# Attention kernel: the sum of a row's squares over the channels as two float32r products with eight columns of weights, in place of one fp32 product

## The chip, the cores and the metric

The kernel runs on one core of a Trainium2 chip. The time is that of the device in microseconds (us), the median over several executions. An execution under the profiler gives the trace that the rows below are read from.

## What is computed

The input `x` has 8 rows of 512 tokens with 512 channels. Each row is layer-normed, goes through gated linear attention with 16 heads and then through a gated MLP, and is multiplied by a gate that a mixture of low-rank experts gives. What the change touches is the second normalization of the attention block:

```
def rmsnorm(x, w, eps=1e-05):
    return x * jax.lax.rsqrt(jnp.mean(x * x, axis=-1, keepdims=True) + eps) * w
...
x = x + o @ Wo
xn2 = rmsnorm(x, ln2_w)
x = x + jax.nn.silu(xn2 @ W1) * (xn2 @ W3) @ W2
```

The mean runs over the 512 channels of each token, here of `x + o @ Wo`.

## The kernel before

Three stages follow each other: F (normalization and experts), A (attention) and M (MLP). Each goes over the 8 rows; on every engine the stage is a first part, a loop and a last body. Activations lie with the channels on the partitions: 128 partitions by 4 blocks of channels by 512 tokens. Most large products are made of float32r operands split in a high and a low part (`..hi`, `..lo`; `product3` at L160 to L162 issues hi·hi, hi·lo, lo·hi). A few small ones are plain fp32; the trace records each of those as two MATMULs.

Stage A walks a row in four chunks of 128 tokens, `c` from 0 to 3. Every engine has its own copy of this order, written by hand, and waits for others on counting semaphores (`count.at(name, i)`: all of row `i`). Pieces of the next row are put between the chunks by `ahead("k0")`, `ahead("q1")` and so on. In the last row (row 7) these pieces are instead those of stage M's beginning (`Front`): for `c` = 3 on ScalarE `third_a`, and on VectorE `weights_lo(dve, 7, 9)` (L1520), which makes two low parts of MLP weights.

The mean of squares, in row `i` for the row before it (whose `x + o @ Wo` lies in `xn`):
- ScalarE squares the four channel blocks (L1190) during chunks 0 to 2, GpSimd adds them into `square` (L1107). `square` and `added` are the first two quarters of the buffer `cum`, under which name the trace shows them.
- TensorE, in chunk 3, after the q1 product of the next row and `variance(i, 2)` (L1303), multiplies `square` by `avg_all`, 128 by 128 with 1/512 everywhere (L1377), into the PSUM region `ms`. Of its 128 equal rows one is read.
- ScalarE makes the inverse root of one partition (`deviation`, L1194 and L1196), SyncE stores it.

Around it, in chunk 3: VectorE first applies the causal mask to both halves of the attention weights (L1022, two instructions), then, once ScalarE has made the inverse deviation of chunk 2, normalizes and gates that chunk's output (`gated`, L1063 to L1070), whose last two steps write the high and low parts `og_hl`. After L1377 TensorE goes on with the state products (L1390) and the products with the masked weights (L1399). The slices of `og_hl` for chunk 3 are free until `gated(i, 3)`, at the end of the row.

Of the kernel before, what the change touches and what calls it, by code (L numbers as in the profile page):

```python
# [5 lines left out]
F32 = mybir.dt.float32  # L6
F32R = mybir.dt.float32r
ALU = mybir.AluOpType
ACT = mybir.ActivationFunctionType
# [4 lines left out]
P = 128  # L14
# [760 lines left out]
def phase_a(nc, outer, consts, f, shared, w, xn_d, r1_d, xmid_d):  # L775
    ident, hmask, causal, avg32, avg_all, ones, eps = consts
    NB, _, KT, T = xn_d.shape
    D = KT * P
    KD = w["wkg2"].shape[1]
    GR = KD // P  # L780
    NC = T // P
# [6 lines left out]
    with ctx:  # L788
        def sb(name, shape, dt=F32):
            return ctx.enter_context(nc.sbuf_tensor("a_" + name, shape, dt))[:]  # L790

        def pair(name, shape):
            return [sb(name + part, shape, F32R) for part in ("hi", "lo")]
# [4 lines left out]
        xn, xa, gsilu = shared  # L798
# [21 lines left out]
        state = [sb(f"state{n}", [P, GR, HG * VH]) for n in range(2)]  # L820
        sq, oc, rn = sb("sq", [P, QD, P]), sb("oc", [P, QD, P]), sb("rn", [P, QD, P])
        og_hl = pair("og", [P, KT, T])
        v_tok = sb("v_tok", [P, NC, D])


        square, added = flat(cum)[:, 0:T], flat(cum)[:, T:2 * T]
# [2 lines left out]
        ps_att = [ctx.enter_context(nc.psum_tensor(f"a_att{n}", [P, 2, GR, 2, P], F32))[:] for n in range(2)]  # L829

        count = Counts(nc, outer, "a")
        for name, per in (("xa_in", 32), ("x2", KT), ("x2sum", KT - 1), ("r2", 1), ("r2_out", 16), ("xn_in", 16), ("xa", KT), ("xahi", KT), ("xalo", KT), ("uhi", 3),
                          ("absz", GR),
                          ("expz", GR), ("softz", GR), ("logg", GR), ("cum", GR * NC), ("offs", 3),
                          ("bias", 1), ("e64", 2), ("e32", 2), ("edk", 1), ("edq", 1), ("ekh", 1), ("eqh", 1),
                          ("decay", 1), ("m64", 3), ("m32", 3), ("mdk", 1), ("mdq", 2), ("mkh", 1), ("mqh", 1),
                          ("state", GR * (NC - 2)), ("first", NC - 1), ("weighing", NC),
                          ("sq", NC), ("rn", NC), ("og", 2 * NC), ("oghi", NC), ("oglo", NC)):
            count.add(name, per)
# [12 lines left out]
        dense = Regions(count, "dense", psum[0:3], sum((results for _, results in order), []), sum(early.values(), []))  # L852
        att = Regions(count, "att", ps_att, [f"{c}_{n}" for c in range(NC) for n in range(2)])
        mix = Regions(count, "mix", psum[3:4], list(range(NC)))
        LAST = KT - 1
        parity, s_parity = sb("parity", [P, 2]), outer.enter_context(nc.semaphore("a_parity"))
        w["ready"] = outer.enter_context(nc.semaphore("aw_ready"))

# [4 lines left out]
        def tokens(c):  # L863
            return slice(c * P, (c + 1) * P)
# [54 lines left out]
        def vector(dve, front):  # L919
# [76 lines left out]
            def clear():  # L996

                dve.tensor_tensor(parity, hmask[:, 0:2], hmask[:, 2:4], ALU.add).then_inc(s_parity, 1)
                dve.wait_ge(s_parity, 1)
                dve.tensor_tensor(parity, parity, hmask[:, 4:6], ALU.add).then_inc(s_parity, 1)  # L1000
                dve.wait_ge(s_parity, 2)
                dve.tensor_tensor(parity, parity, hmask[:, 6:8], ALU.add).then_inc(s_parity, 1)
                dve.wait_ge(s_parity, 3)
                dve.wait_ge(*f.turn.ready(f"xn{LAST}", NB - 1))
                dve.memset(u.bitcast(F32), 0.0)

            def clear_weights():
# [6 lines left out]
            def body(i, ahead):  # L1014
                ahead("split")
                for c in range(NC):
                    if c > 0:
                        dve.wait_ge(*mix.ready(c - 1, i))
                    for n in range(2):
                        dve.wait_ge(*att.ready(f"{c}_{n}", i))  # L1020
                        ps = att.region(f"{c}_{n}").rearrange("p s g o t -> p (s g o) t")
                        dve.tensor_tensor(a_sb[n].rearrange("p s g o t -> p (s g o) t"), ps, bcast(causal, 1, 4 * GR),  # L1022
                                          ALU.mult).then_inc(att.taken_sem(f"{c}_{n}"), 1)
                    ahead(("c0", "u", "c2", "c3")[c])
                    if c + 1 < NC:

                        new, old = state[(c + 1) % 2], state[c % 2]
                        dve.wait_ge(*dense.ready(f"ds{c}", i))
                        ds = dense.region(f"ds{c}")[:, 0:GR * 2 * VH].rearrange("p (g o v) -> p g o v", g=GR, v=VH)
                        for g in range(GR):  # L1030
                            ins = dve.tensor_tensor(new[:, g, :].rearrange("p (h o v) -> p h o v", o=2, v=VH),
                                                    bcast(ds[:, g], 1, HG // 2),
                                                    bcast(hmask.rearrange("p (h o) -> p h o", o=2), 3, VH), ALU.mult)
                            if g == 0:
                                ins.then_inc(count.sem("first"), 1)
                        ins.then_inc(dense.taken_sem(f"ds{c}"), 1)
                        if c > 0:
                            dve.wait_ge(*count.at("first", i, c + 1))
                            dve.wait_ge(*dense.taken(f"ds{c}", i))
                            dve.wait_ge(*count.at("decay", i))  # L1040
                            for g in range(GR):
                                gc = g * NC + c
                                dve.scalar_tensor_tensor(new[:, g, :], old[:, g, :],
                                                                        decay[:, gc:gc + 1], new[:, g, :],
                                                                        ALU.mult, ALU.add).then_inc(count.sem("state"), 1)
                            dve.wait_ge(*count.at("state", i, GR * c))
                    if c > 0:
                        gated(i, c - 1)
                ahead("gates")
                gated(i, NC - 1)  # L1050
                ahead("upper")
                ahead("last")
                ahead("decayed")
                dve.wait_ge(*count.at("xn_in", i))
                for m in range(KT):
                    dve.wait_ge(*dense.ready(f"o{m}", i))
                    dve.tensor_tensor(xn[:, m, :], dense.region(f"o{m}"), xn[:, m, :],
                                                          ALU.add).then_inc(dense.taken_sem(f"o{m}"), 1)
# [54 lines left out]
        def scalar(act, front):  # L1113
# [84 lines left out]
            def body(i, ahead):  # L1198
                ahead("split")
                for c in range(NC):  # L1200
                    if c + 1 < NC:
                        act.wait_ge(*dense.ready(f"kt{c}", i))
                        act.activation(flat(kt_sb), dense.region(f"kt{c}")[:, 0:GR * P],
                                                            ACT.Copy).then_inc(dense.taken_sem(f"kt{c}"), 1)
                    for part in (("k0", "k1"), ("c1",), ("q0",), ("q1",))[c]:
                        ahead(part)
                    if c == 0:
                        act.wait_ge(*dense.taken_before(f"o{LAST}", i))
                    squares(i, ((0, 1), (2,), (3,), ())[c])
                    if c > 0:  # L1210
                        inverse_deviation(i, c - 1)
                    if c == NC - 1:
                        deviation(i)
                    act.wait_ge(*mix.ready(c, i))
                    ps = mix.region(c)
                    act.activation(flat(sq), ps, ACT.Square).then_inc(count.sem("sq"), 1)
                    if c > 0:
                        act.wait_ge(*count.at("og", i, 2 * (c - 1) + 1))
                    act.activation(flat(oc), ps, ACT.Copy).then_inc(mix.taken_sem(c), 1)
                ahead("z")  # L1220
                ahead("v0")
                inverse_deviation(i, NC - 1)
                ahead("exponentials")
                ahead("g")
# [35 lines left out]
        def tensor(pe, front):  # L1260
# [95 lines left out]
            def body(i, ahead):  # L1356
                weights(i, 0)
                for c in range(NC):
# [14 lines left out]
                        variance(i, c - 1)  # L1373
                    if c + 1 == NC:
                        pe.wait_ge(*dense.free("ms", i))
                        pe.wait_ge(*count.at("x2sum", i))
                        pe.matmul(dense.region("ms"), avg_all, square, start=True, stop=True).then_inc(dense.ready_sem("ms"), 1)  # L1377

                    pe.wait_ge(*mix.free(c, i))
                    ps = mix.region(c).rearrange("p (q t) -> p q t", t=P)  # L1380
# [50 lines left out]
                        linear(0, "q", wq, xa_hl, m, first)  # L1431

            f.tensor(pe, first_row)
            for part in ("v0", "v1", "g"):
                parts[part](0)
            loop_parts(pe, NB, parts, body, skip=front.tensor(pe), first=False)
# [552 lines left out]
```

## Time and profile before

| | |
|---|---|
| median of 3 runs | 1624.28 us (1623.22 to 1626.05) |
| time of the profiled execution | 1622.4 us |
| its span in the trace | 1620.7 us |
| TensorE busy | 1593.2 us, 98% |
| VectorE, ScalarE, GpSimd busy | 52%, 35%, 10% |
| granted TensorE clock, mean | 0.998 of full |

A busy share is the part of the span in which the engine had an instruction in flight. The span is the trace's; the time around it is 1.7 us longer. A line number with an engine names a group of instructions; PEld is TensorE's loading of weights, which runs beside its products.

### The profile page before, as it was taken

Reading aid. Unit: us, or ns where it says so; the run is one execution under the profiler, and the core shown is the slowest. Engines: PE = TensorE matmul, PEld = TensorE weight load, DVE = VectorE, ACT = ScalarE, POOL = GpSimd, SP = SyncE. Lnnn points to the kernel's source line nnn. Section 1 sums busy time; section 2 is a strip of 40 time slices with the busy share of each in tenths; the row PEclk is TensorE's granted clock in tenths of the full one; section 3 lists DMA queues with packets and bytes.
Section 4 is the critical chain, followed back from the end, with each engine's and each line's share of the span. In section 5 each row is a group of like instructions: output and inputs, shape, how many; then the busy total and the mean of one; then the engine's idle time right before and its main releaser. Section 6 shows DMA issues by size and latency. Waiting matters only on the chain.

```text
span 1620.7 us, 30581 instructions
## 1 busy us (share of the span) xinstructions
PE 1593.2 (98%) x12274; PEld 1277.6 (79%) x12274; DVE 847.3 (52%) x1311; ACT 567.2 (35%) x982; POOL 167.2 (10%) x190
## 2 busy tenths in 40 slices
PE   7999999999999999999999999999999999999998
PEld 5777888777777777777777788888888888888886
DVE  5565455367797887978876451331415142241413
ACT  4333343366564645636564411111111111111111
POOL 4770000100220102101020000000000000000000
PEclk9999999999999999999999999999999999999999
DMA  7563332101020210202213423030301203030200
GB/s 175 151 135 78 83 95 69 59 27 52 9 84 0 84 53 32 84 0 84 84 54 118 144 101 127 0 136 0 136 0 49 87 0 136 0 136 0 91 14 26
DMA packets 50700, 113.16 MB, mean 70 GB/s; under 512 B 13321, under 2 KB 24665, under 8 KB 42466
## 3 DMA queue, kind: packets, MB, share of 16 engines
q1 hardware_dynamic: 47906, 99.95, 19.5%
q10 hardware_dynamic: 1152, 8.39, 1.3%
q0 software_dynamic: 1600, 4.25, 0.9%
q8 instruction: 28, 0.46, 0.1%
q14 instruction: 14, 0.11, 0.0%
HBM read 78.98 MB, written 33.59 MB: 69 GB/s over the span
## 4 chain that ended last, share of the span: by engine, by line
PE 94%; DVE 2%; ACT 1%; issue 1%; DMA 1%; PEld 0%; SPq 0%; ACTq 0%; DVEq 0%; PEldq 0%
PE m_ps L1529 10%; PE m_ps L1531 10%; PE m_ps L1530 10%; PE a_ps L160 7%; PE a_ps L162 7%; PE a_ps L161 7%; PE f_ps L160 5%; PE f_ps L162 5%; PE f_ps L161 5%; PE m_ps L1543 5%; PE m_ps L1544 5%; PE m_ps L1545 5%; PE a_att L1282 3%; PE a_ps L1399 2%; PE a_ps L1303 2%; PE a_ps L1390 1%
## 5 line engine op out<-in xcount | busy, mean ns | idle before, releaser
L1529 PE MATMUL m_ps<-m_xshi,m_w 128*128 128x512 f32 x680 | 268.1, 394 | 1.4 <-DVE m_w L1520 1.4
L1766 DVE TENSOR_TENSOR m_h<-m_ps,m_silu 128x512 f32<-128x512 f32 x85 | 58.7, 690 | 402.4 <-PE m_ps L1531 402.4
L1531 PE MATMUL m_ps<-m_xshi,m_w 128*128 128x512 f32 x680 | 266.5, 392 | 0.0
L1530 PE MATMUL m_ps<-m_xslo,m_w 128*128 128x512 f32 x680 | 266.4, 392 | 0.0
L1830 ACT ACTIVATE m_silu<-m_ps 128x512 f32<-128x512 f32 x85 | 50.8, 597 | 334.3 <-PE m_ps L1531 334.3
L1529 PEld LDWEIGHTS m_ps<-m_xshi,m_w 128*128 128x128 f32 x680 | 127.7, 188 | 30.0 <-issue 2.1
L1531 PEld LDWEIGHTS m_ps<-m_xshi,m_w 128*128 128x128 f32 x680 | 127.6, 188 | 28.7
L1530 PEld LDWEIGHTS m_ps<-m_xslo,m_w 128*128 128x128 f32 x680 | 127.7, 188 | 28.1 <-issue 0.2
L1101 POOL TENSOR_TENSOR row<-row,a_r 128x512 f32<-128x512 f32 x32 | 50.7, 1615 | 331.6 <-DMA a_r<-scratch_r 331.6
L1022 DVE TENSOR_TENSOR a_a<-a_att,causal 128x1024 f32<-128x1024 f32 x64 | 75.2, 1216 | 11.8 <-PE a_att L1282 11.8
L1839 ACT ACTIVATE m_h0hi<-m_h 128x512 fp32r<-128x512 f32 x46 | 29.1, 632 | 135.7 <-DVE m_h L1766 135.7
L1543 PE MATMUL m_ps<-m_h0hi,m_w 128*128 128x512 f32 x192 | 75.3, 392 | 0.0
L1544 PE MATMUL m_ps<-m_h0lo,m_w 128*128 128x512 f32 x192 | 75.3, 392 | 0.0
L1545 PE MATMUL m_ps<-m_h0hi,m_w 128*128 128x512 f32 x192 | 75.3, 392 | 0.0
L1839 ACT ACTIVATE m_h1hi<-m_h 128x512 fp32r<-128x512 f32 x39 | 24.7, 632 | 115.6 <-DVE m_h L1766 115.6
L1107 POOL TENSOR_TENSOR a_cum<-a_cum 128x512 f32<-128x512 f32 x24 | 30.7, 1281 | 321.3 <-ACT a_cum L1190 321.3
L1543 PE MATMUL m_ps<-m_h1hi,m_w 128*128 128x512 f32 x160 | 62.6, 391 | 0.0
L1544 PE MATMUL m_ps<-m_h1lo,m_w 128*128 128x512 f32 x160 | 62.6, 391 | 0.0
L1545 PE MATMUL m_ps<-m_h1hi,m_w 128*128 128x512 f32 x160 | 62.6, 391 | 0.0
L160 PE MATMUL f_ps<-f_xnhi,f_w1hi 128*128 128x512 f32 x128 | 52.1, 407 | 2.5 <-DVE f_xnlo L476 1.2
L160 PE MATMUL a_ps<-a_wvhi,a_xahi 128*128 128x512 f32 x128 | 53.1, 415 | 0.0
L160 PE MATMUL a_ps<-a_xahi,a_wghi 128*128 128x512 f32 x128 | 50.8, 397 | 0.9 <-ACT a_v_tok L1149 0.6
(306 smaller groups left out, 3487.9 us busy)
## 6 DMA issues: line engine op xcount, KB each, us to landing
row<-scratch_xn SPq DMA_DIRECT2D x16, 1024.0 KB, 4.9
row<-scratch_xmid SPq DMA_DIRECT2D x16, 1024.0 KB, 7.3
m_xt<-in_L_attn_W SPq DMA_DIRECT2D x33, 256.0 KB, 3.2
f_xt<-in_L_attn_x SPq DMA_DIRECT2D x32, 256.0 KB, 8.1
scratch_xn<-row SPq DMA_DIRECT2D x8, 1024.0 KB, 9.0
scratch_gate<-row ACTq DMA_DIRECT2D x8, 1024.0 KB, 3.9
scratch_xmid<-row SPq DMA_DIRECT2D x8, 1024.0 KB, 3.9
row<-scratch_gate SPq DMA_DIRECT2D x8, 1024.0 KB, 10.5
```

The costliest lines, as they stand in the source:

```text
L160: pe.matmul(out, lh, rh, start=first and n == 0, stop=False)
L161: pe.matmul(out, lh, rl, start=False, stop=False)
L162: ins = pe.matmul(out, ll, rh, start=False, stop=last and n == end)
L1022: dve.tensor_tensor(a_sb[n].rearrange("p s g o t -> p (s g o) t"), ps, bcast(causal, 1, 4 * GR), ALU.mult).then_inc(att.taken_sem(f"{c}_{n ...
L1529: pe.matmul(ps, wh, xh, start=k == 0, stop=False)
L1530: pe.matmul(ps, wh, xl, start=False, stop=False)
L1531: ins = pe.matmul(ps, wl, xh, start=False, stop=k == LAST)
L1543: pe.matmul(ps, lh, rh, start=j == 0, stop=False)
L1544: pe.matmul(ps, lh, rl, start=False, stop=False)
L1545: ins = pe.matmul(ps, ll, rh, start=False, stop=j == FT - 1)
L1766: dve.tensor_tensor(h[n], dense.region(f"b{j}"), silu[n], ALU.mult).then_inc(dense.taken_sem(f"b{j}"), 1)
L1839: act.activation(h_hl[n][0], h[n], ACT.Copy).then_inc(count.sem("hhi"), 1)
```

## The change

The product is made of float32r operands (the parts of the diff in their order: VectorE's setup `clear`, VectorE's body, ScalarE's, TensorE's, TensorE ahead of its loop). ScalarE copies `square` to a float32r high part (`x2hi`), VectorE subtracts it from `square` into a low part (`x2lo`); both go to the unused slices of `og_hl`. TensorE multiplies each by `mean8`, 128 by 8 with 1/512 everywhere, and adds both in eight rows of the same PSUM region. `mean8` is set once by VectorE at the start of stage A. TensorE's wait for `x2sum` becomes a wait for `x2lo`.

```
+        mean8 = sb("mean8", [P, 8], F32R)
...
             def clear():
...
+                dve.memset(mean8.bitcast(F32), 1.0 / D).then_inc(s_mean8, 1)
...
                     ahead(("c0", "u", "c2", "c3")[c])
+                    if c == NC - 1:
+                        dve.wait_ge(*count.at("x2hi", i))
+                        dve.tensor_tensor(og_hl[1][:, :, tokens(c)], square.rearrange("p (m t) -> p m t", t=P),
+                                          og_hl[0][:, :, tokens(c)].bitcast(F32), ALU.subtract).then_inc(count.sem("x2lo"), 1)
...
+                    if c == NC - 1:
+                        act.wait_ge(*count.at("x2sum", i))
+                        act.activation(og_hl[0][:, :, tokens(c)], square, ACT.Copy).then_inc(count.sem("x2hi"), 1)
                     for part in (("k0", "k1"), ("c1",), ("q0",), ("q1",))[c]:
                         ahead(part)
...
                     if c + 1 == NC:
                         pe.wait_ge(*dense.free("ms", i))
-                        pe.wait_ge(*count.at("x2sum", i))
-                        pe.matmul(dense.region("ms"), avg_all, square, start=True, stop=True).then_inc(dense.ready_sem("ms"), 1)
+                        pe.wait_ge(*count.at("x2lo", i))
+                        ps = dense.region("ms")[0:8]
+                        pe.matmul(ps, mean8, og_hl[0][:, :, tokens(c)], start=True, stop=False)
+                        pe.matmul(ps, mean8, og_hl[1][:, :, tokens(c)], start=False, stop=True).then_inc(dense.ready_sem("ms"), 1)
...
             f.tensor(pe, first_row)
+            pe.wait_ge(s_mean8, 1)
```

How the instructions stand now in chunk 3, with the line numbers of the changed program. On TensorE in the loop, from the end of the q1 product on; L1314 is the variance of chunk 2 (L1303 before), L1403 and L1412 are the state products and those with the masked weights. Before:

```order
L162 MATMUL a_ps<-a_xahi,a_wqlo 128x512
L1303 MATMUL a_ps<-a_sq,avg 128x512
L1377 MATMUL a_ps<-a_cum,avg_all 128x512
L1390 MATMUL a_ps<-a_neg,a_state 128x128 x4
L1399 MATMUL a_ps<-a_a,a_v_tok 32x128 x16
```

And now:

```order
L162 MATMUL a_ps<-a_xahi,a_wqlo 128x512
L1314 MATMUL a_ps<-a_sq,avg 128x512
L1389 MATMUL a_ps<-a_oghi,a_mean 8x512
L1390 MATMUL a_ps<-a_oglo,a_mean 8x512
L1403 MATMUL a_ps<-a_neg,a_state 128x128 x4
L1412 MATMUL a_ps<-a_a,a_v_tok 32x128 x16
```

The two products stand where the one stood, with the wait for `x2lo` ahead of both of them and everything else behind.

On VectorE in the last row, chunk 3, in the changed program; L1026 is the mask, L1534 the low part of MLP weights (L1520 before), L1031 the new subtraction, L1071 to L1078 `gated`:

```order
L1026 TENSOR_TENSOR a_a<-a_att,causal 128x1024 x2
L1534 TENSOR_TENSOR m_w<-m_xt,m_w 128x512 x2
L1031 TENSOR_TENSOR a_oglo<-a_cum,a_oghi 128x4x128
L1071 TENSOR_TENSOR a_rn<-a_rn,a_oc 128x512
L1074 TENSOR_TENSOR a_rn<-a_rn,row 128x512
L1076 CAST a_oghi<-a_rn 128x4x128
L1078 TENSOR_TENSOR a_oglo<-a_rn,a_oghi 128x4x128
```

The subtraction is behind the masks in every row, and in this one also behind two instructions on weights; in the loop nothing stands between L1026 and L1031.

On ScalarE in the loop, chunk 3; L1230 is the last instruction of chunk 2 (L1219 before), L1215 the new copy, L1137 the q1 result, L1242 and L1244 the inverse deviation of chunk 2, L1202 and L1204 `deviation`:

```order
L1230 ACTIVATE a_oc<-a_ps 128x512
L1215 ACTIVATE a_oghi<-a_cum 128x4x128
L1137 ACTIVATE a_q<-a_ps 128x512
L1242 ACTIVATE a_rn<-a_ps,eps 128x512
L1244 ACTIVATE a_rn<-a_rn 128x512
L1202 ACTIVATE a_cum<-a_ps,eps 1x512
L1204 ACTIVATE a_cum<-a_cum 1x512
```

The copy stands ahead of the q1 result.

## Rows read from the trace of the kernel before

**Rows 1.** The page, busy time of each engine.
```profile
PE 1593.2 (98%) x12274; PEld 1277.6 (79%) x12274; DVE 847.3 (52%) x1311; ACT 567.2 (35%) x982; POOL 167.2 (10%) x190
```
**Rows 2.** The page, chain that ended last, share by engine.
```profile
PE 94%; DVE 2%; ACT 1%; issue 1%; DMA 1%; PEld 0%; SPq 0%; ACTq 0%; DVEq 0%; PEldq 0%
```
**Rows 3.** Windows (us): busy time by engine, granted clock (PEclk), DMA share, GB/s.
```profile
461.00:530.00 69.00, 69.00 (x941) 54.02 (x940) 56.33 (x75) 37.78 (x67) 10.04 (x7) 1.00 0.13 49
896.30:899.00 2.70, 1.29 (x6) 0.99 (x6) 1.82 (x3) 2.37 (x4) 0.00 (x0) 1.00 0.62 185
```
**Rows 4.** TensorE's waits: us in total, times, longest us.
```profile
PE m_ps L1529 <- DVE m_w L1520: 1.4, 1, 1.4
...
PE a_ps L160 <- ACT a_v_tok L1149: 0.6, 2, 0.5
...
PE a_ps L160 <- ACT row L1181: 0.3, 1, 0.3
```
**Rows 5.** Timeline, row 1, chunk 3: start us, us, engine, what [idle before].
```profile
459.78 0.60 ACT L1219 ACTIVATE a_oc<-a_ps 128x512 f32<-128x512 f32 x1 [0.91 <-DVE a_rn L1063]
460.97 0.69 DVE L1070 TENSOR_TENSOR a_oglo<-a_rn,a_oghi 128x512 fp32r<-128x512 f32 x1
461.58 2.35 DVE L1022 TENSOR_TENSOR a_a<-a_att,causal 128x1024 f32<-128x1024 f32 x2
462.68 1.02 PE L1303 MATMUL a_ps<-a_sq,avg 128*128 128x512 f32 x2
462.88 0.60 ACT L1129 ACTIVATE a_q<-a_ps 128x512 f32<-128x512 f32 x1 [2.50 <-PE a_ps L162]
463.54 1.02 PE L1377 MATMUL a_ps<-a_cum,avg_all 128*128 128x512 f32 x2
464.39 1.05 PE L1390 MATMUL a_ps<-a_neg,a_state 128*128 128x128 f32 x8
464.99 0.66 ACT L1194 ACTIVATE a_cum<-a_ps,eps 1x512 f32<-1x512 f32 x1
465.12 0.69 DVE L1063 TENSOR_TENSOR a_rn<-a_rn,a_oc 128x512 f32<-128x512 f32 x1 [1.19 <-ACT a_rn L1233]
```
**Rows 6.** Timeline, row 1: the last addition of squares.
```profile
456.35 1.28 POOL L1107 TENSOR_TENSOR a_cum<-a_cum 128x512 f32<-128x512 f32 x1 [8.53 <-ACT a_cum L1190]
```
**Rows 7.** Timeline, row 1: float32r products with 48 and 16 columns of weights.
```profile
446.03 0.39 PE L1320 MATMUL a_ps<-a_xalo,a_wkg 128*16 128x512 f32 x1
446.26 0.40 PE L1318 MATMUL a_ps<-a_xahi,a_wkg 128*48 128x512 f32 x1
446.26 0.09 PEld L1320 LDWEIGHTS a_ps<-a_xalo,a_wkg 128*16 128x16 f32 x1
446.50 0.39 PE L1320 MATMUL a_ps<-a_xalo,a_wkg 128*16 128x512 f32 x1
```
**Rows 8.** Timeline, stage F: TensorE waits for VectorE, then runs float32r products.
```profile
14.35 0.68 DVE L476 TENSOR_TENSOR f_xnlo<-row,f_xnhi 128x512 fp32r<-128x512 f32 x1
15.09 0.19 PEld L160 LDWEIGHTS f_ps<-f_xnhi,f_w1hi 128*128 128x128 f32 x1 [0.70 <-DVE f_xnlo L476]
15.09 0.50 PE L160 MATMUL f_ps<-f_xnhi,f_w1hi 128*128 128x512 f32 x1 [0.27 <-DVE f_xnlo L476]
15.43 0.39 PE L161 MATMUL f_ps<-f_xnlo,f_w1hi 128*128 128x512 f32 x1
15.66 0.40 PE L162 MATMUL f_ps<-f_xnhi,f_w1lo 128*128 128x512 f32 x1
```
**Rows 9.** Timeline, rows 0 and 6: mask and product (x8 pairs in all).
```profile
393.49 2.35 DVE L1022 TENSOR_TENSOR a_a<-a_att,causal 128x1024 f32<-128x1024 f32 x2
395.42 1.02 PE L1377 MATMUL a_ps<-a_cum,avg_all 128*128 128x512 f32 x2
...
793.62 2.35 DVE L1022 TENSOR_TENSOR a_a<-a_att,causal 128x1024 f32<-128x1024 f32 x2
795.52 1.02 PE L1377 MATMUL a_ps<-a_cum,avg_all 128*128 128x512 f32 x2
```
**Rows 10.** Timeline, row 7 (the last), chunk 3.
```profile
865.07 1.28 DVE L1520 TENSOR_TENSOR m_w<-m_xt,m_w 128x512 fp32r<-128x512 f32 x2
866.81 0.69 DVE L1063 TENSOR_TENSOR a_rn<-a_rn,a_oc 128x512 f32<-128x512 f32 x1 [0.46 <-ACT a_rn L1233]
...
864.56 1.02 PE L1377 MATMUL a_ps<-a_cum,avg_all 128*128 128x512 f32 x2
865.42 1.05 PE L1390 MATMUL a_ps<-a_neg,a_state 128*128 128x128 f32 x8
```

More of the change, by code:

```diff
@@ L831, in phase_a @@
         count = Counts(nc, outer, "a")
-        for name, per in (("xa_in", 32), ("x2", KT), ("x2sum", KT - 1), ("r2", 1), ("r2_out", 16), ("xn_in", 16), ("xa", KT), ("xahi", KT), ("xalo", KT), ("uhi", 3),
+        for name, per in (("xa_in", 32), ("x2", KT), ("x2sum", KT - 1), ("x2hi", 1), ("x2lo", 1), ("r2", 1), ("r2_out", 16), ("xn_in", 16), ("xa", KT), ("xahi", KT), ("xalo", KT), ("uhi", 3),
                           ("absz", GR),
@@ L855, in phase_a @@
         LAST = KT - 1
+        s_mean8 = outer.enter_context(nc.semaphore("a_mean8"))
         parity, s_parity = sb("parity", [P, 2]), outer.enter_context(nc.semaphore("a_parity"))
```

## The prediction

> **What bounds the kernel now.** I read the page first: busy time, then the chain of work that ended last. TensorE is busy for 98% of the span [rows 1] and makes 94% of the chain [rows 2]. Next the window of one whole row of stage A: TensorE busy for 69.00 of 69.00 us at full clock, VectorE for 56.33 and ScalarE for 37.78 [rows 3]. In the table of TensorE's waits no entry names L1377 or its neighbours; those of stage A's rows are small and in row 0 [rows 4]. So in every row TensorE sets the pace, a piece of work taken off it is won in full, and a wait put into it is lost in full, unless TensorE has later to wait for something that isn't itself late. What counts is therefore when the new wait is met. That is read from the timeline of chunk 3.
>
> **What is removed.** The fp32 product is two MATMULs; the first starts at 463.54 and what follows it at 464.39, so it holds TensorE for 0.85 us [rows 5], eight times in the kernel (eight rows).
>
> **What is added on TensorE.** Two float32r products of 512 columns. The nearest rows are those of L1318 and L1320, with 48 and 16 columns of weights: they start 0.23 to 0.24 us apart [rows 7], whatever the number of weight columns. Two of them in a dense stream would take 0.46 us, 0.39 less than before. That alone would give 8 x 0.39 = 3.1 us.
>
> The Trainium skill ("TensorE: Matmul & The Clock Gate", Back-to-back issue gap) puts the gap at N/2.4 + 2.5 ns, 216 ns for 512 columns. The trace says 0.23 for N = 512, and the measurement decides; by the page's figure the sum would be 8 x 2 x 0.015, about 0.2 us, lower. Its section LDWEIGHTS puts a load at columns/1.2, some 7 ns for eight columns, where the row of a 16-column load shows 0.09 us.
>
> **What the new wait costs.** Four steps.
> 1. The sum of squares is there early: GpSimd's last addition ends at 456.35 + 1.28 = 457.63 [rows 6], six us ahead of its use. The wait removed was met long before.
> 2. ScalarE's copy to the high part stands ahead of the q1 result. ScalarE ends chunk 2 at 459.78 + 0.60 = 460.38 and then is idle for 2.50 us until the q1 product is ready [rows 5]. A copy of about 0.6 us (as its neighbours on 128x512) lies in that gap and costs nothing; it ends near 461.0. If the gap were gone it would delay the q1 result by 0.6 us, which TensorE doesn't wait for here.
> 3. VectorE's subtraction stands behind both masks. Those run from 461.58 for 2.35 us, to 463.93 [rows 5]. L1070, a subtraction of the same shape and types, takes 0.69. VectorE starts an instruction between 0.08 us before the end of the one before (461.58 against 460.97 + 0.69 [rows 5]) and some 0.03 after it; I take 0.03 before. The low part is ready at 463.90 + 0.69 = 464.59. VectorE itself loses nothing, since it is idle for 1.19 us before L1063 [rows 5].
> 4. TensorE comes to the product at 463.54 and finds the low part missing. In stage F such a wait ends 0.06 us after VectorE does (14.35 + 0.68 = 15.03 against 15.09), and the first product then holds TensorE for 0.34 us, not 0.23, as its weights are loaded in the open (0.19 us) [rows 8]. Here the load is that of eight columns, nearer to the 0.09 of rows 7, so I take 0.29; the bounds are 0.23 and 0.34. The pair starts at 464.65 and what follows it at 464.65 + 0.29 + 0.23 = 465.17, where before it was 464.39: **0.78 us later**. Both products wait, the one on the high part too, since the wait stands ahead of both.
>
> With both ends of steps 3 and 4 a row costs 0.67 to 0.89 us. This was row 1, where the masks end 0.39 us after L1377 starts. In rows 0 and 6 it is 0.42 (393.49 + 2.35 against 395.42) and 0.45 [rows 9]; over the seven rows 0 to 6 the mean is 0.42. So a row costs 0.81 on average (0.70 to 0.92), **seven rows 5.7 us** (4.9 to 6.4).
>
> **The last row** is another case. There the subtraction stands also behind L1520, which makes parts of MLP weights until 865.07 + 1.28 = 866.35 [rows 10]. Low part at 866.32 + 0.69 = 867.01, TensorE starts at 867.07, what follows comes at 867.59, before 865.42: **2.2 us** (2.1 to 2.3). L1063, which started at 866.81, is put off to about 867.05; it feeds the end of the row, which is later by then anyway.
>
> **What else is late, and who waits.** Behind the waiting product stand L1390, L1399, then z, v, g and the output product of the row: all of TensorE's work. ScalarE's `deviation` (464.99 [rows 5]) now waits for the product's result, which comes at about 465.3, and is through long before the next result of TensorE, itself 0.8 us later. The other engines follow TensorE from there, so nothing catches up. The memset of `mean8` (eight columns, once, in stage A's setup) and the eight copies on ScalarE are hidden.
>
> **The sum.** 5.7 + 2.2 = +7.9 us (7.0 to 8.7). The profiled execution took 1622.4 us, which makes 1630.3 (1629.4 to 1631.1). It was 1.9 us quicker than the median of the runs shown; by that median, 1624.28, the time is **1632.2 us** (1631.3 to 1633.0), slower by 0.49%. A measurement of this kernel can tell about 0.2%, 3.2 us, from no change.
>
> **The rivals.**
> - *Given back in part* (0.13). Row 0 has TensorE waits of 0.6 and 0.3 us for ScalarE, and stage M's first body one of 1.4 for weights [rows 4]. If what ends them doesn't move with TensorE, they swallow up to 2.3 of the 7.9: +5.6, 1629.9. Against it: those chains begin with TensorE's own results in the same row.
> - *Knock-on at the seam or elsewhere* (0.10). The last row's 2.2 us come where weights are loaded, halved and stored in a hand-written order; another wait of 2 to 3 us behind them gives about +10.5, 1634.8.
> - *The wait is hidden* (0.05; the other side). If the low part is there when TensorE arrives, only the gain is left: 8 x 0.39 = 3.1 us, 1621.2, at the edge of what can be told from no change. It decides at 463.54 in row 1: the subtraction would have to end 1.05 us sooner than worked out, as by VectorE taking it ahead of the masks. In the order of VectorE it stands behind them, and the masks alone end later than that.
> - *The clock falls in the new gaps* (0.04). The gaps are 1.1 us, one of 2.5. In 896.3 to 899, with 1.4 us of waiting, the granted clock stays at 1.00, which is 2.4 GHz [rows 3]. No row of stage A is at 1.2 GHz. Ten 512-column products at half speed behind each gap would add 10 x 0.23 x 8 = 18 us: 1650. The same page of the skill says that an idle engine is put to half clock; after gaps of this size the trace doesn't show it.
> - *float32r at fp32's pace* (0.02). The change would do nothing on TensorE: the pair would hold it for 4 x 0.43 us, +10 us more, 1642. Rows 7 speak against it.
> - My forecast has the rest, 0.66.
>
> **How the numbers follow.** The likeliest case's own range is 1629.5 to 1634, its bounds and the 1 us by which medians of runs differ from each other. With the partial give-back and the knock-on taken in, 1628.5 to 1635 leaves out under 2 in 10. Slower by over 0.2% are the forecast, the give-back, the knock-on, the clock and the pace, 0.95 together, less 0.02 for a give-back of more than is worked out: 0.93. The hidden wait's 0.05 lies at the edge: 0.02 of it go to faster by over 0.2%, the rest with the 0.02 to within 0.2%, 0.05.
>
> **What the profile after would show.** L1389 in TensorE's waits, eight times, released by VectorE's L1031, seven of 1.1 us and one of 2.5. Its start 0.06 us after L1031 ends. L1031 starting where L1026 ends, 0.69 long. L1215 in ScalarE's gap, with L1137 no later against TensorE than before. Distances of TensorE work unchanged everywhere else: a row of stage A takes 0.8 us more, stage M the same. Wrong would be: no wait at L1389 (VectorE done sooner), a row that is longer by other than the wait less 0.33, or waits of rows 4 that shrink.

## The result and the profile after

The changed kernel takes 1631.69 us (median of 6 runs, 1630.40 to 1637.38) against 1624.37 (6 runs, 1623.22 to 1626.09): 1.0046 times, 95% interval 1.0036 to 1.0056, which is 5.8 to 9.1 us more. The forecast was 7.9 us more.

Page of the changed kernel, busy time of each engine:

```profile
PE 1592.0 (98%) x12274; PEld 1275.2 (78%) x12274; DVE 855.1 (52%) x1320; ACT 572.7 (35%) x990; POOL 162.8 (10%) x190
```

TensorE has as many instructions as in [rows 1], 1.2 us less to do, and a span of 1630.7 instead of 1620.7 us. So the time is not in work. TensorE's table of waits (us in total, times, longest us), changed kernel:

```profile
PE a_ps L1389 <- DVE a_oglo L1031: 9.4, 8, 2.4
...
PE m_ps L1543 <- DVE m_w L1534: 1.6, 1, 1.6
...
PE a_ps L160 <- ACT a_v_tok L1157: 0.6, 2, 0.5
PE a_ps L160 <- ACT row L1189: 0.3, 1, 0.3
```

The first line is new: the first float32r product waits for VectorE's subtraction in each of the eight rows. The other three are those of [rows 4], and none has shrunk; that of stage M's weights is 1.6 instead of 1.4 us. The table counts a wait from the end that it shows for the product before. For L1314 that is 1.02 us after its start, though the next product could start after 0.86, so the first line's 9.4 us are 0.16 us a row less than TensorE loses.

Timeline of row 1, chunk 3, changed kernel, to be held against [rows 5]:

```profile
463.37 0.62 ACT L1215 ACTIVATE a_oghi<-a_cum 128x512 fp32r<-128x512 f32 x1
...
464.67 2.35 DVE L1026 TENSOR_TENSOR a_a<-a_att,causal 128x1024 f32<-128x1024 f32 x2
...
465.76 1.02 PE L1314 MATMUL a_ps<-a_sq,avg 128*128 128x512 f32 x2
...
466.94 0.68 DVE L1031 TENSOR_TENSOR a_oglo<-a_cum,a_oghi 128x512 fp32r<-128x512 f32 x1
467.74 0.09 PEld L1389 LDWEIGHTS a_ps<-a_oghi,a_mean 128*8 128x8 f32 x1 [1.79 <-issue]
467.77 0.39 PE L1389 MATMUL a_ps<-a_oghi,a_mean 128*8 128x512 f32 x1 [0.99 <-DVE a_oglo L1031]
467.77 0.09 PEld L1390 LDWEIGHTS a_ps<-a_oglo,a_mean 128*8 128x8 f32 x1
467.99 0.40 PE L1390 MATMUL a_ps<-a_oglo,a_mean 128*8 128x512 f32 x1
468.20 0.69 DVE L1071 TENSOR_TENSOR a_rn<-a_rn,a_oc 128x512 f32<-128x512 f32 x1 [0.57 <-ACT a_rn L1244]
468.23 1.06 PE L1403 MATMUL a_ps<-a_neg,a_state 128*128 128x128 f32 x8
```

The subtraction begins when the masks end (464.67 + 2.35 = 467.02) and is done at 467.62. TensorE, which would have got to the product at 465.76 + 0.86 = 466.62, starts it at 467.77. The state products come 2.47 us after the variance (L1314) instead of 1.71 (464.39 - 462.68 in [rows 5]): 0.76 us lost, which is 1.15 of waiting less 0.39 won on the product. VectorE's idle time ahead of L1071 has gone from 1.19 to 0.57 us and isn't used up.

The last row, changed kernel, against [rows 10]:

```profile
870.36 2.35 DVE L1026 TENSOR_TENSOR a_a<-a_att,causal 128x1024 f32<-128x1024 f32 x2
871.26 1.02 PE L1314 MATMUL a_ps<-a_sq,avg 128*128 128x512 f32 x2
872.62 1.28 DVE L1534 TENSOR_TENSOR m_w<-m_xt,m_w 128x512 fp32r<-128x512 f32 x2
873.82 0.69 DVE L1031 TENSOR_TENSOR a_oglo<-a_cum,a_oghi 128x512 fp32r<-128x512 f32 x1
...
874.65 0.39 PE L1389 MATMUL a_ps<-a_oghi,a_mean 128*8 128x512 f32 x1 [2.37 <-DVE a_oglo L1031]
...
875.11 1.06 PE L1403 MATMUL a_ps<-a_neg,a_state 128*128 128x128 f32 x8
```

Here the two instructions on MLP weights stand between masks and subtraction, and the state products come 3.85 us after the variance (875.11 - 871.26) instead of 1.71: 2.14 us lost.

The profiled execution took 1632.75 us, 10.35 more than that of before. Of these, 2.20 lie before chunk 3 of row 0 (variance at 396.76 against 394.56), 7.49 between there and the state products of the last row (875.11 - 396.76 against 865.42 - 394.56), and the remaining 0.66 behind these and outside the span. The 7.49 are what the change does, and the medians moved by 7.3; the 2.2 are taken up under what stays open.

### The profile page after: what moved, and what is told of

Same layout as the page of the kernel before. It is cut to its first block and busy times, and to the rows that moved or that the text cites. A ratio compares the mean times of both kernels' runs of the same rounds, so it can differ in the third digit from the quotient of the medians.

```text
span 1630.7 us, 30608 instructions
## 1 busy us (share of the span) xinstructions
PE 1592.0 (98%) x12274; PEld 1275.2 (78%) x12274; DVE 855.1 (52%) x1320; ACT 572.7 (35%) x990; POOL 162.8 (10%) x190
## 5 line engine op out<-in xcount | busy, mean ns | idle before, releaser
L1026 DVE TENSOR_TENSOR a_a<-a_att,causal 128x1024 f32<-128x1024 f32 x64 | 75.2, 1218 | 12.1 <-PE a_att L1293 12.1
L160 PE MATMUL f_ps<-f_xnhi,f_w1hi 128*128 128x512 f32 x128 | 52.0, 406 | 2.9 <-DVE f_xnlo L476 1.9
L160 PE MATMUL a_ps<-a_wvhi,a_xahi 128*128 128x512 f32 x128 | 53.2, 416 | 0.0
L160 PE MATMUL a_ps<-a_xahi,a_wghi 128*128 128x512 f32 x128 | 50.8, 396 | 0.9 <-ACT a_v_tok L1157 0.6
```

What stands on the lines that cost most here:

```text
L160: pe.matmul(out, lh, rh, start=first and n == 0, stop=False)
```

## The experiments

Every experiment was timed beside the kernel before. "Step" is the distance from one row's first state product to the next one's, the mean over the steps between rows 1 and 6, from the timelines; "last step" is that from row 6 to row 7, which holds the beginning of stage M too. The step is 66.40 us in the kernel before.

| kernel | ratio to before, 95% | step | last step |
|---|---|---|---|
| before | 1 | 66.40 | 69.05 |
| the changed one | 1.0046 (1.0036 to 1.0056) | 67.16 | 71.10 |
| e1_sub_first | 0.9979 (0.9970 to 0.9988) | 66.01 | 69.37 |
| e2_wait_only | 1.0068 (1.0056 to 1.0080) | 67.61 | 71.70 |
| e3_sub_before_weights | 1.0045 (1.0031 to 1.0058) | 67.17 | 69.64 |
| e4_fp32_8_columns | 1.0013 (1.0004 to 1.0022) | 66.67 | 68.96 |
| e5_high_only | 0.9979 (0.9970 to 0.9988) | 65.97 | 69.14 |
| e6_sub_twice | 1.0089 (1.0075 to 1.0102) | 67.88 | 72.04 |
| e7_pool_split | 1.0025 (1.0015 to 1.0035) | 66.86 | 69.69 |
| e8_128_columns | 0.9977 (0.9968 to 0.9985) | 65.99 | 68.57 |
| e9_copy_behind_q1 | 1.0061 (1.0046 to 1.0075) | 67.33 | 71.12 |

**The subtraction ahead of the masks** (e1_sub_first).

```
             def body(i, ahead):
...
+                    if c == NC - 1:
+                        dve.wait_ge(*count.at("x2hi", i))
+                        dve.tensor_tensor(og_hl[1][:, :, tokens(c)], square.rearrange("p (m t) -> p m t", t=P),
+                                          og_hl[0][:, :, tokens(c)].bitcast(F32), ALU.subtract).then_inc(count.sem("x2lo"), 1)
                     for n in range(2):
                         dve.wait_ge(*att.ready(f"{c}_{n}", i))
...
                     ahead(("c0", "u", "c2", "c3")[c])
-                    if c == NC - 1:
-                        dve.wait_ge(*count.at("x2hi", i))
-                        dve.tensor_tensor(og_hl[1][:, :, tokens(c)], square.rearrange("p (m t) -> p m t", t=P),
-                                          og_hl[0][:, :, tokens(c)].bitcast(F32), ALU.subtract).then_inc(count.sem("x2lo"), 1)
```

> The changed kernel with VectorE's subtraction moved ahead of the two masks of chunk 3 (in the last row so ahead of the MLP weights too). Theory A (the whole loss is TensorE's wait for the low part, which is late only because it stands behind the masks): no wait at the product in any row, eight times 0.39 us won, about 1621.2 against 1624.3 of before, ratio 0.998; the masks end 0.69 later, at about 0.2 us ahead of the products that need them. Theory B (the two products or the copies cost as such, in the engines' other work): it stays within 2 us of the changed kernel, 1630 to 1632. Theory C (the masks, put off by 0.69 us, become the next wait): a wait at L1412 of 0.2 to 0.7 us a row, 1623 to 1627.

Measured: 1622.99 us beside 1626.40, ratio 0.9979, faster than both kernels. Timeline of row 0, e1_sub_first (L1025 is the subtraction, L1030 the masks):

```profile
399.28 0.68 DVE L1025 TENSOR_TENSOR a_oglo<-a_cum,a_oghi 128x512 fp32r<-128x512 f32 x1
399.89 2.35 DVE L1030 TENSOR_TENSOR a_a<-a_att,causal 128x1024 f32<-128x1024 f32 x2
...
400.27 1.02 PE L1314 MATMUL a_ps<-a_sq,avg 128*128 128x512 f32 x2
...
401.60 1.06 PE L1403 MATMUL a_ps<-a_neg,a_state 128*128 128x128 f32 x8
...
402.58 1.08 PE L1412 MATMUL a_ps<-a_a,a_v_tok 128*32 128x128 f32 x32
```

No wait is left; the state products come 1.33 us after the variance where it was 1.71, so the gain of 0.38 us is there in full, and the step is shorter by 0.39. The masks end at 402.24, 0.34 us ahead of L1412, which needs them. That is little: with masks more than 0.34 us later, TensorE would wait there instead. Theory A holds, B and C fall.

**The wait without the new products** (e2_wait_only). High and low part are made and waited for, but not used.

```
                         pe.wait_ge(*count.at("x2lo", i))
-                        ps = dense.region("ms")[0:8]
-                        pe.matmul(ps, mean8, og_hl[0][:, :, tokens(c)], start=True, stop=False)
-                        pe.matmul(ps, mean8, og_hl[1][:, :, tokens(c)], start=False, stop=True).then_inc(dense.ready_sem("ms"), 1)
+                        pe.matmul(dense.region("ms"), avg_all, square, start=True, stop=True).then_inc(dense.ready_sem("ms"), 1)
```

> The changed kernel, high and low parts made and the low part waited for, but the product is the fp32 one of before. Theory A (wait and product add up): seven rows of 1.15 us and one of 2.5, +10.6 us, about 1635 against 1624.3, ratio 1.0065; the difference to the changed kernel is the gain of the products, 3.1 us. Theory B (the loss comes from the new products): close to before, 1624 to 1626.

Measured: 1.0068, +11.1 us; the step is 1.21 us over before. The wait alone costs more than the whole change, and the products win part of it back (1.21 - 0.76 = 0.45 a row). Theory A. The 0.45 are more than the 0.39 of a product without a wait. The timeline of row 1 shows why, e2_wait_only:

```profile
467.86 1.10 PE L1388 MATMUL a_ps<-a_cum,avg_all 128*128 128x512 f32 x2 [0.98 <-DVE a_oglo L1031]
...
468.80 1.05 PE L1401 MATMUL a_ps<-a_neg,a_state 128*128 128x128 f32 x8
```

Behind a wait the fp32 product holds TensorE for 0.94 us, not 0.85.

**The subtraction ahead of the weights** (e3_sub_before_weights).

```
+                    if c == NC - 1:
+                        dve.wait_ge(*count.at("x2hi", i))
+                        dve.tensor_tensor(og_hl[1][:, :, tokens(c)], square.rearrange("p (m t) -> p m t", t=P),
+                                          og_hl[0][:, :, tokens(c)].bitcast(F32), ALU.subtract).then_inc(count.sem("x2lo"), 1)
                     ahead(("c0", "u", "c2", "c3")[c])
-                    if c == NC - 1:
-                        dve.wait_ge(*count.at("x2hi", i))
-                        dve.tensor_tensor(og_hl[1][:, :, tokens(c)], square.rearrange("p (m t) -> p m t", t=P),
-                                          og_hl[0][:, :, tokens(c)].bitcast(F32), ALU.subtract).then_inc(count.sem("x2lo"), 1)
```

> The changed kernel with the subtraction behind the masks but ahead of the piece of the next part (the MLP weights in the last row; nothing in the others). Theory A: only the last row's wait shrinks, from 2.4 to about 1.1 us, so 1.3 us less than the changed kernel, about 1630.4, ratio to before 1.0038. Theory B (the last row's extra wait is covered further on by the wait for MLP weights): the same time as the changed kernel, 1631.7.

Measured: 1.0045 (1.0031 to 1.0058). The 1.3 us are 0.0008 of the time and can't be told by the ratio. The trace can: the step is unchanged, the last step is 1.46 us shorter. TensorE's wait, e3_sub_before_weights:

```profile
PE a_ps L1389 <- DVE a_oglo L1030: 8.1, 8, 1.2
```

The longest wait has gone from 2.4 to 1.2 us and the sum from 9.4 to 8.1; the last row's state products come 2.65 us after the variance instead of 3.85, 1.20 sooner. The other 0.26 of the last step are pauses of TensorE with no releaser in the trace (0.92 us in that step instead of 1.20), and not the change. The last row's larger loss came from the weights standing in front.

**The fp32 product with eight columns** (e4_fp32_8_columns), from the kernel before.

```
-                        pe.matmul(dense.region("ms"), avg_all, square, start=True, stop=True).then_inc(dense.ready_sem("ms"), 1)
+                        pe.matmul(dense.region("ms")[0:8], avg_all[:, 0:8], square, start=True, stop=True).then_inc(dense.ready_sem("ms"), 1)
```

> The kernel before with the same fp32 product, but only eight of the 128 columns of weights. If the number of weight columns doesn't set the time of a product, the next instruction starts 0.85 us later as before and the time is 1624.3 (ratio 1.000). If the weight load counts (two loads of 0.19 against 0.09), up to 0.2 us a row, 1622.7.

Measured: 1.0013, slower by 0.7 to 3.6 us, and the step is 0.28 longer. Neither expectation had that sign. Timeline of row 0, e4_fp32_8_columns:

```profile
394.39 1.02 PE L1303 MATMUL a_ps<-a_sq,avg 128*128 128x512 f32 x2
395.34 0.10 PEld L1377 LDWEIGHTS a_ps<-a_cum,avg_all 128*8 128x8 f32 x2 [0.76 <-issue]
395.34 1.03 PE L1377 MATMUL a_ps<-a_cum,avg_all 128*8 128x512 f32 x2
...
396.29 0.97 PEld L1390 LDWEIGHTS a_ps<-a_neg,a_state 128*128 128x128 f32 x8 [0.86 <-issue]
396.29 1.16 PE L1390 MATMUL a_ps<-a_neg,a_state 128*128 128x128 f32 x8
```

The weights of L1377 are loaded 0.95 us behind L1303's start, at the moment at which the product itself starts; before, the first load lies 0.43 us behind L1303's start, under the running product. Those of L1390 are late likewise: 1.90 us from the variance to the state products, not 1.71. The rest of the 0.28 lies in the state products, 1.16 us long instead of 1.05. Why the loads aren't made earlier, no run shows.

**Only the high part** (e5_high_only). The low part is left out, so the mean is that of the rounded squares.

```
-                        pe.wait_ge(*count.at("x2lo", i))
+                        pe.wait_ge(*count.at("x2hi", i))
                         ps = dense.region("ms")[0:8]
-                        pe.matmul(ps, mean8, og_hl[0][:, :, tokens(c)], start=True, stop=False)
-                        pe.matmul(ps, mean8, og_hl[1][:, :, tokens(c)], start=False, stop=True).then_inc(dense.ready_sem("ms"), 1)
+                        pe.matmul(ps, mean8, og_hl[0][:, :, tokens(c)], start=True, stop=True).then_inc(dense.ready_sem("ms"), 1)
```

> The changed kernel without the low part: VectorE's subtraction and the second product are left out, so the mean of squares is that of the rounded high part. Theory A: ScalarE's copy is there 2.5 us ahead of the product, no wait, one product of 0.23 in place of 0.85 us, 0.62 us a row, 5.0 us under before, 1619.3, ratio 0.997. If the copy itself cost something on the path, or TensorE lost elsewhere, it would be over 1621.

Measured: 0.9979, no better than e1_sub_first. At the spot itself the gain is complete, and row 1 shows 1.09 us from variance to state products. But the step is shorter by 0.43, not 0.62. What is new in its table of weight-load waits over 465 to 531 us, e5_high_only:

```profile
PEld a_ps L160 <- ACT row L1185: 0.4, 1, 0.4
PEld a_ps L160 <- DVE a_neg L948: 0.2, 1, 0.2
```

L1185 is ScalarE's gate (L1181 before), which frees a PSUM region that TensorE's next products need. In the kernel before rows 1 to 6 have neither line. TensorE is now far enough ahead to run into ScalarE. The missing 0.19 us are lost at that spot, as TensorE's products there show, row 1, e5_high_only:

```profile
487.57 0.40 PE L162 MATMUL a_ps<-a_xahi,a_wglo 128*128 128x512 f32 x1
487.88 0.19 PEld L160 LDWEIGHTS a_ps<-a_xahi,a_wghi 128*128 128x128 f32 x1 [0.36 <-ACT row L1185]
487.89 0.50 PE L160 MATMUL a_ps<-a_xahi,a_wghi 128*128 128x512 f32 x1
...
488.22 0.40 PE L161 MATMUL a_ps<-a_xalo,a_wghi 128*128 128x512 f32 x1
```

From L162 to L161 it takes 0.65 us instead of 0.46 (two distances of 0.23). Counted from the row's first state product, TensorE's order is that of the kernel before up to here, and 0.19 us behind it from here on. No run took this wait away.

**The subtraction twice** (e6_sub_twice), the second waiting for the first.

```
-        for name, per in (... ("x2hi", 1), ("x2lo", 1), ...
+        for name, per in (... ("x2hi", 1), ("x2lo", 2), ...
...
                     if c == NC - 1:
                         dve.wait_ge(*count.at("x2hi", i))
                         dve.tensor_tensor(og_hl[1][:, :, tokens(c)], square.rearrange("p (m t) -> p m t", t=P),
                                           og_hl[0][:, :, tokens(c)].bitcast(F32), ALU.subtract).then_inc(count.sem("x2lo"), 1)
+                    if c == NC - 1:
+                        dve.wait_ge(*count.at("x2lo", i, 1))
+                        dve.tensor_tensor(og_hl[1][:, :, tokens(c)], square.rearrange("p (m t) -> p m t", t=P),
+                                          og_hl[0][:, :, tokens(c)].bitcast(F32), ALU.subtract).then_inc(count.sem("x2lo"), 1)
```

> The changed kernel with VectorE's subtraction done twice, the second waiting for the first. Theory A (TensorE waits for the end of the subtraction, one for one): 0.69 to 0.75 us more in each of eight rows, 5.5 to 6 us over the changed kernel, 1637.4. But L1071 on VectorE then also starts later, as its idle time was 0.57 us, with nobody waiting for it. Theory B (TensorE's loss has another releaser, such as a queue): less than 3 us more.

Measured: 1.0089, and a step 0.72 us over the changed kernel's. TensorE's wait, e6_sub_twice:

```profile
PE a_ps L1393 <- DVE a_oglo L1035: 15.2, 8, 3.1
```

5.8 us more in eight rows, 0.72 each: TensorE follows the end of the subtraction one for one. Theory A. The last row shows something else too. Its gap is now 3.26 us, and behind it TensorE's clock falls (the second block is a window: behind the busy times of TensorE, its loads, VectorE, ScalarE and GpSimd come the granted clock, the DMA share and GB/s):

```profile
879.75 0.44 PE L1393 MATMUL a_ps<-a_oghi,a_mean 128*8 128x512 f32 x1 [3.10 <-DVE a_oglo L1035]
...
880.41 1.91 PE L1407 MATMUL a_ps<-a_neg,a_state 128*128 128x128 f32 x8
```

```profile
880.00:883.00 3.00, 3.00 (x26) 2.63 (x28) 2.01 (x4) 1.31 (x2) 0.00 (x0) 0.50 0.00 0
```

A granted clock of 0.50 is 1.2 GHz, and the state products take 1.91 us instead of 1.06.

**Both parts on GpSimd** (e7_pool_split). The high part is one more addition ahead of GpSimd's last one, the low part a subtraction behind it. VectorE's subtraction and ScalarE's copy are gone.

```
                     pool.wait_ge(*count.at("x2", i, m + 1))
+                    if m == LAST:
...
+                        pool.tensor_tensor(hi, whole, last, ALU.add).then_inc(count.sem("x2hi"), 1)
+                        pool.wait_ge(*count.at("x2hi", i))
                     pool.tensor_tensor(square, square, added, ALU.add).then_inc(count.sem("x2sum"), 1)
+                pool.wait_ge(*count.at("x2sum", i))
+                pool.tensor_tensor(lo, whole, hi.bitcast(F32), ALU.subtract).then_inc(count.sem("x2lo"), 1)
```

> The changed kernel with both parts made by GpSimd right after its additions (three additions or subtractions of 1.28 us from 456.4 on in the numbers of row 1, ready at about 460.2, 3.3 us ahead of the product); ScalarE and VectorE have nothing new. Theory A (GpSimd's idle time is free): 3.1 us under before, 1621.2. Theory C (GpSimd slows VectorE, as in the trace of before, where L961 takes 2.31 us beside GpSimd's scaling and 1.22 without): the state update and the gating in 458.1 to 460.2 take up to 1.1 us more each, the masks end 1 to 2 us later, and TensorE waits at the products that need them, 1625 to 1635.

Measured: 1.0025, slower than before although the product never waits. Timeline of row 0, e7_pool_split:

```profile
394.03 1.26 POOL L1117 TENSOR_TENSOR a_cum<-a_cum 128x512 f32<-128x512 f32 x1
394.38 2.62 DVE L1047 SCALAR_TENSOR_TENSOR a_state<-a_state,a_decay 128x256 f32<-128x256 f32 x2
395.37 1.35 POOL L1119 TENSOR_TENSOR a_oglo<-a_cum,a_oghi 128x512 fp32r<-128x512 f32 x1
...
402.05 1.08 PE L1413 MATMUL a_ps<-a_a,a_v_tok 128*32 128x128 f32 x32 [0.87 <-DVE a_a L1026]
```

VectorE's state update takes 2.62 us beside GpSimd's additions; in the kernel before, the same two instructions (L1043) take 0.88. So the masks are late, and TensorE waits for them at L1413: 0.87 us here, 0.75 to 0.80 in rows 1 to 6, 1.20 in the last. Less the 0.39 won on the product, that is the 0.46 us by which the step is longer. Theory C: the engine that looked free wasn't, since it slows the one whose results are due next. In the kernel before, GpSimd's last addition is over (457.63 in row 1) when the state update begins (458.14); whether a place in GpSimd's order exists at which nothing is slowed wasn't tried.

**All 128 columns** (e8_128_columns), from e1_sub_first, `avg_all` read as float32r in place of `mean8`.

```
-                        ps = dense.region("ms")[0:8]
+                        ps, mean = dense.region("ms"), avg_all.bitcast(F32R)
```

> e1_sub_first with the two float32r products made with all 128 columns of weights (the existing avg_all read as float32r), in place of eight. Theory A (a float32r product takes 0.23 us whatever the columns, and the gain is that of float32r alone): the state products start 1.32 us after the variance in every row, as in e1_sub_first, and the time is that of e1_sub_first, ratio 0.998. If the eight columns bring something: up to 0.2 us a row slower, ratio 0.999.

Measured: 0.9977 (0.9968 to 0.9985), step 65.99 us: that of e1_sub_first. Timeline of row 1, e8_128_columns:

```profile
464.63 1.02 PE L1314 MATMUL a_ps<-a_sq,avg 128*128 128x512 f32 x2
...
465.95 1.05 PE L1403 MATMUL a_ps<-a_neg,a_state 128*128 128x128 f32 x8
```

1.32 us from one to the other. The eight columns bring nothing; the gain is that of float32r alone.

**The copy behind the q1 result** (e9_copy_behind_q1), from the changed kernel.

```
-                    if c == NC - 1:
-                        act.wait_ge(*count.at("x2sum", i))
-                        act.activation(og_hl[0][:, :, tokens(c)], square, ACT.Copy).then_inc(count.sem("x2hi"), 1)
                     for part in (("k0", "k1"), ("c1",), ("q0",), ("q1",))[c]:
                         ahead(part)
+                    if c == NC - 1:
+                        act.wait_ge(*count.at("x2sum", i))
+                        act.activation(og_hl[0][:, :, tokens(c)], square, ACT.Copy).then_inc(count.sem("x2hi"), 1)
```

> The changed kernel with ScalarE's copy to the high part behind the q1 result instead of ahead of it, so that it ends 1.2 us after the q1 product, about 0.2 us after the masks end. Theory A (the copy was hidden in ScalarE's idle time, with about 2.9 us to spare before the subtraction): the subtraction now waits for it, 0.2 to 0.4 us more a row, none in the last row if VectorE's weights cover it, or 1 us there since the copy then stands behind the weights' high parts; 1.5 to 3.5 us over the changed kernel, ratio 1.006. Theory B (ScalarE has no part in it): the same as the changed kernel, 1.0046.

Measured: 1.0061 (1.0046 to 1.0075), whose interval overlaps that of the changed kernel; the trace tells the two apart. The step is 0.17 us over the changed kernel's, and the last row has nothing more (3.86 us from the variance to the state products against 3.85). Timeline of row 1, e9_copy_behind_q1:

```profile
466.85 2.35 DVE L1026 TENSOR_TENSOR a_a<-a_att,causal 128x1024 f32<-128x1024 f32 x2
...
468.62 0.62 ACT L1217 ACTIVATE a_oghi<-a_cum 128x512 fp32r<-128x512 f32 x1
469.28 0.69 DVE L1031 TENSOR_TENSOR a_oglo<-a_cum,a_oghi 128x512 fp32r<-128x512 f32 x1
```

The copy now ends at 469.24, 0.04 us after the masks, and the subtraction starts at 469.28 instead of 469.12. In the changed kernel the copy ended at 463.99, 2.95 us ahead of the subtraction: it was hidden, as forecast.

## Why the prediction was right

The mechanism is the one forecast, and each of its steps can be set beside a row.

- *What bounds the kernel.* TensorE paces every row, and what delays it is lost in full. Shown by e6_sub_twice, where 0.69 us put on VectorE behind the masks gives 0.72 us a row, and by e1_sub_first, where 0.38 us taken off TensorE shortens the step by 0.39. e5_high_only shows where this ends: of 0.62 us won a row only 0.43 arrive.
- *The gain of the products,* 0.39 us a row: 0.38 in e1_sub_first. Right, but the cause is only the float32r format, as e8_128_columns shows.
- *Steps 1 and 2, sum and copy hidden:* right. In row 1 of the changed kernel GpSimd's last addition ends at 460.72, 2.65 us ahead of the copy, and the copy 2.95 us ahead of the subtraction; only when e9_copy_behind_q1 puts it behind the masks does it cost.
- *Step 3, the subtraction behind the masks:* right. It started 0.08 us before the masks' end, which was the lower bound and not the 0.03 I took, and lasted 0.68.
- *Step 4, TensorE's start and the pair:* right to 0.02 us by luck, since errors cancel. TensorE started 0.15 us after the subtraction's end (467.77 against 467.62), where I had 0.06 from stage F; and the pair took 0.46 us with no extra for weights loaded in the open (the first product 0.22), where I had 0.52. With the subtraction's start in step 3, 0.05 us sooner than taken, it is in sum 0.76 us in row 1 against 0.78. The 0.15 could have been read beforehand: in the kernel before, TensorE's L1529 starts at 897.87, 0.15 us after VectorE's L1520, which starts at 897.03 and takes 0.69.
- *Seven rows:* 5.35 us against 5.7, from the distance of the variances of rows 0 and 7 (871.26 - 396.76 against 863.71 - 394.56). That is 0.76 a row; I had added 0.03 for the later masks of other rows. In the changed kernel the masks of rows 1 to 6 all end 0.40 or 0.41 us after TensorE could have started the product, and only row 0 has more (0.51, and 0.86 us lost).
- *The last row:* 2.14 against 2.2, and e3_sub_before_weights takes 1.20 of it back.
- *The sum:* 7.5 against 7.9, and the medians give 7.3 (5.8 to 9.1 by the ratio's interval).

Of the rivals, the give-back has no trace in the changed kernel: the waits of [rows 4] are 0.6, 0.3 and 1.6 us, where they were 0.6, 0.3 and 1.4. It does show in e5_high_only in the other direction, where TensorE is ahead of its time. The knock-on didn't come: behind the last row's state products the trace is 0.3 to 0.4 us longer. The hidden wait is what e1_sub_first builds; it needed another place in VectorE's order, and gave 3.4 us (1.9 to 4.9) where 3.1 were forecast. The clock: in the window of a whole row of the changed kernel, with its gap of 1 us, and in that of the last row's gap of 2.5 us, it stays at 1.00 (behind the busy times of TensorE, its loads, VectorE, ScalarE and GpSimd come the granted clock, the DMA share and GB/s; changed kernel):

```profile
467.00:535.00 68.00, 66.25 (x931) 52.09 (x932) 54.93 (x75) 38.64 (x69) 10.12 (x7) 1.00 0.13 50
863.00:876.00 13.00, 10.63 (x214) 7.97 (x212) 12.20 (x19) 8.08 (x14) 1.28 (x1) 1.00 0.17 43
```

Behind the gap of 3.26 us in e6_sub_twice the clock did fall, so this rival was a real one; there only one gap is that long, where the 18 us that I had for it counted all eight.

float32r at fp32's pace is ruled out by the 0.22 and 0.24 us at which L1389 and L1390 are followed.

**What stays open.** In the profiled executions of the nine kernels with the new parts of the sum, the variance of row 0 starts between 396.1 and 400.3 us; in the two without them (before and e4_fp32_8_columns) at 394.6 and 394.4. The traces show three parts in this. Stage A's first product is already late, by 0.94 us in the changed kernel (343.27 against 342.33) and by up to 3.0 us in the others. This comes from stage F and is there before the change does anything: TensorE's L691 (the group near 194 us) starts at 194.21 instead of 193.32, 0.89 of the 0.94 us, and `mean8` is set at 289.95. Then TensorE pauses once, for 1.15 to 1.5 us, at about 385 to 389 us where the trace names no releaser, in the changed kernel, e1, e2, e3, e7 and e9. And in e1, e7 and e8 the granted clock is 0.50 for a while behind TensorE's 1.6 us wait at about 370 us, which the other kernels have too, at a clock of 1.00; it costs about 1.6 us. Pause and half clock don't belong to the new parts as such: e5_high_only and e6_sub_twice have these parts and take 52.2 us from stage A's first product to the variance, as before. The profiled executions also differ from the medians: that of before took 2.0 us less than its median, that of e4 4.4 less, and that of e1, whose variance is latest, 2.9 more. And the timed executions leave no room for a late start: for e1_sub_first the eight rows are worth 3.1 us (8 x 0.39) and the ratio gives 3.4, where a start later by 5.7 us, as in its profile, would have made it slower than before. Why stage F is later, what makes the pause, and why it comes in some of the kernels alone, wasn't tried.

The last step varies too. TensorE pauses in it once or twice, for 0.9 to 1.7 us in all (1.38 before, 1.20 in the changed kernel, 1.72 in e1), again with no releaser. e1_sub_first's last step is 0.3 us longer than before where it should be 0.4 shorter; half of this difference is pauses, the other half isn't explained.

## What to carry to other kernels

Where an in-order engine is full, making one of its instructions cheaper pays only if its new operand is ready by the time it is reached: here 0.39 us of product were won and 1.15 of waiting lost, and one line moved ahead of 2.35 us of other work on VectorE turned +7.3 us into about -3.4. Read for each new operand where its maker stands in its own engine's order, in the last or first iteration too, where other pieces stand between. And an idle engine is not a free one: 2.6 us of GpSimd's additions made the two VectorE instructions beside them three times as long.

## What the runs showed of the hardware

- An fp32 product of 512 columns with 8 columns of weights holds TensorE for longer than one with 128: 0.95 us against 0.85. The fp32 product ahead of it is followed later too, after 0.95 instead of 0.86, so that the state products come 1.90 us after the variance instead of 1.71. Its weight load starts together with it, 0.95 us behind the start of the product before, where that of 128 columns starts after 0.43 (e4_fp32_8_columns). In float32r 8 and 128 columns take the same (1.33 and 1.32 us from variance to state products).
- TensorE's start after another engine's result isn't one number: 0.06 us in stage F [rows 8], and also in stage A of the kernel before (L160 at 368.30, behind VectorE's L923, whose first instruction ends at 368.24); 0.15 at L1389 in all eight rows, and at L1529 in the kernel before (897.87 behind 897.72). What makes the difference isn't shown; it isn't the stage or the loop, since L1389 has 0.15 in the last body too.
- A weight load of eight columns that stands in the open, after a wait, adds nothing to see: 467.74 and 467.77 are the starts of load and product, and the next product comes 0.22 us later. With 128 columns the first product in stage F held 0.34 [rows 8], and the fp32 one of e2_wait_only 0.94 instead of 0.85. By the Trainium skill ("TensorE: Matmul & The Clock Gate", LDWEIGHTS) a load takes columns/1.2 ns, which makes an estimate of 7 ns for eight columns. The trace's rows of such a load show 0.09 us, and the measurement decides.
- Beside GpSimd's additions, two VectorE instructions on operands in SBUF took 2.62 instead of 0.88 us.
- After a gap in TensorE's work the clock can fall to half: behind 3.26 us in the last row of e6_sub_twice the granted clock was 0.50. Behind 1.15 and 2.5 us in the changed kernel it stayed at 1.00. The wait of 1.6 us at the start of stage A had both: 1.00 in the kernel before, 0.50 behind it in e1, e7 and e8.
